# Expert stage of an attention and mixture-of-experts layer: the transposes of a tile's gated rows move behind the gate products of the next tile

## What is computed

```python
g = jnp.einsum('td,edf->etf', x, w_gate)
u = jnp.einsum('td,edf->etf', x, w_up)
h = jax.nn.silu(g) * u
down = jnp.einsum('etf,efd->etd', h, w_down)
routed = jnp.einsum('te,etd->td', gates, down)
shared = jax.nn.silu(x @ sw_gate) * (x @ sw_up) @ sw_down
out = routed + shared
```

## Time and profile before

| | us |
|---|---|
| median of 3 runs | 2293.08 |
| lowest, highest | 2290.29, 2299.49 |
| profiled execution | 2301.97 |
| its span, first to last instruction | 2300.3 |
| TensorE busy in the span | 2139.7 (93%) |
| VectorE busy | 1483.7 (64%) |
| ScalarE busy | 1034.7 (45%) |
| mean granted TensorE clock | 0.974 of full speed |

### The profile page before, as it was taken

One profiled execution on the slowest core, in us unless ns is written; L12 is line 12 of the kernel. 1 busy time (PEld: TensorE's weight loads), 2 busy tenths in 40 slices (PEclk: granted clock), 3 DMA queues, 4 the chain that ended last, 5 costly groups with the idle time before them and its releaser, 6 DMA issues. The chain is left out here.

```text
span 2300.3 us, 32737 instructions
## 1 busy us (share of the span) xinstructions
PE 2139.7 (93%) x11865; PEld 1389.3 (60%) x11865; DVE 1483.7 (64%) x3323; ACT 1034.7 (45%) x1924; POOL 1168.6 (51%) x717
## 2 busy tenths in 40 slices
PE   6999899999999999999999988699998899999997
PEld 5777544444444444444444432577776798999896
DVE  3665786767767677777777760765657556565654
ACT  3333255555555555555555555322222334443433
POOL 1010166557465674656746557455563345465554
PEclk9999799999999999999999999899999899999999
DMA  5678711412213122161231200344432676767673
GB/s 169 233 264 257 194 31 38 93 33 69 67 38 93 29 67 72 38 153 29 68 71 38 73 17 19 124 147 129 147 111 80 235 242 196 237 227 249 215 225 115
DMA packets 172913, 283.69 MB, mean 123 GB/s; under 512 B 28622, under 2 KB 75214, under 8 KB 172752
## 3 DMA queue, kind: packets, MB, share of 16 engines
q1 hardware_dynamic: 151488, 219.09, 32.5%
q0 software_dynamic: 21264, 62.51, 8.2%
HBM read 196.22 MB, written 86.90 MB: 123 GB/s over the span
## 5 line engine op out<-in xcount | busy, mean ns | idle before, releaser
L931 ACT ACTIVATE b_pt<-b_st 128x512 f32<-128x512 f32 (+3 forms) x1280 | 612.5, 535 | 472.7 <-DVE b_st L893 187.6
L752 POOL TENSOR_TENSOR b_acc<-b_acc,b_pt 128x1024 f32<-128x1024 f32 (+1 forms) x256 | 592.9, 2346 | 214.3 <-ACT b_pt L931 213.7
L871 DVE TENSOR_REDUCE b_mpart<-b_mx 128x1 f32<-128x512 f32 x768 | 512.1, 686 | 184.8 <-PE b_mx L988 182.1
L1011 PE MATMUL b_st<-b_q,b_k 97*128 97x512 f32 (+2 forms) x1280 | 497.4, 402 | 57.5 <-ACT b_pt L931 54.0
L988 PE MATMUL b_mx<-b_k,b_q 96*128 96x512 f32 (+2 forms) x1280 | 508.9, 412 | 6.9 <-DVE b_mpart L871 3.3
L988 PEld LDWEIGHTS b_mx<-b_k,b_q 96*128 96x128 f32 x1280 | 248.4, 195 | 262.0 <-DVE b_mpart L871 148.9
L1011 PEld LDWEIGHTS b_st<-b_q,b_k 97*128 97x128 f32 x1280 | 242.3, 191 | 262.7 <-ACT b_pt L931 237.4
L1024 PE MATMUL b_ob<-b_pt,b_v 128*32 128x512 f32 (+3 forms) x2560 | 303.6, 547 | 1.1 <-ACT b_pt L931 1.1
L868 DVE CUSTOM_DVE_ANT_0 b_unread<-b_mx,b_later 128x384 bf16<-128x384 f32 (+3 forms) x512 | 244.5, 484 | 87.0 <-PE b_mx L988 86.3
L752 POOL TENSOR_TENSOR b_acc<-b_pt 128x1024 f32<-128x1024 f32 x48 | 113.5, 2379 | 263.0 <-ACT b_pt L931 263.0
L80 PE MATMUL c_fb<-e_w_split,e_xh 128*128 128x352 f32 x408 | 142.3, 349 | 1.4 <-DVE e_xl L1727 1.4
(11 more groups left out here) (296 smaller groups left out, 3818.0 us busy)
## 6 DMA issues: line engine op xcount, KB each, us to landing
b_q<-scr_qh SPq DMA_DIRECT2D x64, 256.0 KB, 4.5
b_k<-scr_kh SPq DMA_DIRECT2D x64, 256.0 KB, 4.1
sw_raw<-in_L_ffn_w_gate_dram SPq DMA_DIRECT2D x14, 704.0 KB
sw_raw<-in_L_ffn_w_up_dram SPq DMA_DIRECT2D x14, 704.0 KB
c_x_rows<-in_L_ffn_w_gate_dram SPq DMA_DIRECT2D x13, 704.0 KB
c_x_rows<-in_L_ffn_w_up_dram SPq DMA_DIRECT2D x13, 704.0 KB
a_xin<-in_L_attn_x_dram POOLq DMA_DIRECT2D x8, 1024.0 KB, 5.8
scr_qh<-wo SPq DMA_DIRECT2D x8, 1024.0 KB, 5.0
```

The lines of the kernel that those rows point to most:

```text
L752: g.tensor_tensor(out[:, :, lo:], so_far[:, :, lo:], pt[n % NPB][:, :, lo:], ALU.add).then_inc(s_add, 1)
L871: v.tensor_reduce(part, mxb[i % NMX][:, 0:w], AX.X, ALU.max).then_inc(s_red, 1)
L931: act.activation(pt[n % NPB][:, j, lo:], stb[:, (2 * n + j) % NST, lo:], ACT.Exp, scale=SCALE).then_inc(s_exp, 1)
L1011: pe.matmul(stb[:, (2 * n + j) % NST, lo:], kb[:, h, at:at + P], qb[:, h, q * CH + lo:(q + 1) * CH], start=True, stop=True).then_inc(s_st, 1)
```

## The change

The transposes of the gated rows of tile i-1 are issued behind the gate product of tile i, ahead of the transposes of the input rows of tile i+1, and no longer ahead of that gate product. For the last tile they stand where they stood. ScalarE's silu of tile i waits in addition for c_hf of tile i-1, and the gate product of tile i waits in addition for silu of tile i-1. No instruction is added or removed. Line numbers behind the edits are up to 6 higher.

```diff
         for i in range(UNITS):
             act.wait_ge(s_g, i + 1)
+            if i:
+                act.wait_ge(s_h, i)
             act.activation(sg, gb[:, 0:F], ACT.Silu).then_inc(s_sg, 1)
...
         for i in range(UNITS):
             pe.wait_ge(s_xl, i + 1)
+            if i:
+                pe.wait_ge(s_sg, i)
             hidden(gb, i, 0).then_inc(s_g, 1)
+            if i:
+                turn_hidden(i - 1)
             if i + 1 < UNITS:
                 pe.wait_ge(s_x[(i + 1) % UNDER_WAY], turns(i + 1, UNDER_WAY))
                 turn_row(pe, begun, keep, i + 1).then_inc(s_t, 1)
             hidden(ub, i, 1).then_inc(s_u, 1)
             if i:
                 down_row(i - 1)
-            turn_hidden(i)
+        turn_hidden(UNITS - 1)
         down_row(UNITS - 1)
```

## The result

| | before | after |
|---|---|---|
| median of five runs, us | 2293.08 | 2315.51 |
| lowest, highest | 2290.29, 2299.49 | 2309.01, 2324.65 |
| profiled execution: time, span | 2301.97, 2300.3 | 2324.65, 2322.9 |
| expert stage in the profile (first gate product to last down product) | 498.4 | 521.9 |

The account below looks back on a forecast made before the run. TensorE was taken to bound the expert stage. New waits of 30.3 us, less 7.5 gone, plus 0.7 at tile 6, gave 23.5 us longer: 2316.6 us on the median, range 2301 to 2334.

Parts of the forecast that it names:

- both pieces: Tiles with both late weight pieces and one addition: slack 0.53 to 0.57, each 1.44 short, 7.2 us of new waits.
- three additions: Six tiles with three additions and an up piece: slack 0.3 to 1.0, together 7.6 us of new waits.
- two additions and a piece: Five tiles with two additions and a down piece: slack 1.45, short by 0.56 each, 2.8 us of new waits.
- five others: Tiles 27, 49, 66, 68 and 70: slack 1.2 to 1.8, together 3.0 us of new waits.
- seven with late output rows: Tiles 15, 19, 26, 37, 48, 52, 59, where an addition waits for output rows: 9.7 us of new waits.
- Tile 6: Tile behind the one wait for a weight transfer: e_xl ends at 1836.7, making it 0.7 us longer.
- The waits gone: TensorE's waits for c_hf at nine places besides tile 6 vanish, saving about 7.5 us.
- The waits only go: VectorE catches up between c_hl and e_xl; c_hf waits vanish, none come: near -6, 2287 us; chance 0.04.
- Under half of it: Output rows' arrivals don't move and each shift is 0.3 us smaller: about +9, 2302 us; chance 0.09.
- The clock falls at seven transposes in a row: TensorE product takes 3.56 us instead of 2.00 in up to 70 tiles: +109, 2402 us; chance 0.02.
- Weights come late as well: Weight fetches, issued about 2 us later, bring 12 more waits of 2: +24 more, 2341 us; chance 0.05.
- It does nothing: The change has no effect because e_xl is not on the chain; chance 0.02.

Follow-up runs that it names:

- e6: Changed kernel with the gated rows' transposes behind 3 of the gate product's 12 matmuls; ratio 1.0009 to the kernel before.
- e7: Kernel before with only the two added waits, transposes in their old place; ratio 0.9981 to the kernel before.
- e12: Kernel before with only the weight pieces of the block of index 3 split two tiles later; ratio 0.9965 to the kernel before.
- e5: Changed kernel with the gated rows' transposes behind 6 of the gate product's 12 matmuls; ratio 1.0007 to the kernel before.
- e8: Changed kernel with additions and late pieces behind e_xl, and block 3's pieces two tiles later; ratio 0.9981 to the kernel before.

## Why the prediction was right, point by point

**Right in its mechanism and its sum, partly by compensation.** The waits moved from c_hf to e_xl, and the undisturbed tile did not change. By the steps of the prediction, in us of waits for e_xl, start to start:

| kind of tile | forecast | measured |
|---|---|---|
| both pieces (five) | 7.2 | 7.0 |
| three additions (six) | 7.6 | 6.0 |
| two additions and a piece (five) | 2.8 | 2.6 |
| five others | 3.0 | 1.1 |
| seven with late output rows | 9.7 | 8.3 |
| together | 30.3 | 25.0 |

- *Five others* was mis-sized: tiles 27, 49 and 66 do not wait. In the trace of the kernel before, c_hh of the tile but one before had started 1.40, 1.61 and 0.90 us after its transposes, on an idle ScalarE, and not 0.53. So the slack was read too small by 0.87, 1.08 and 0.37. The line for tile 27, whose transposes start at 1977.88:

```profile
1979.28 0.49 ACT L2015 ACTIVATE c_hh<-e_tb 128x384 fp32r<-128x384 f32 x1 [3.35 <-PE e_tb L2065]
```

  In the changed kernel these three start at the usual distance, and e_xl is 0.25, 0.25 and 0.18 us early, as a slack of 2.2 less 2.00 says. There the semaphore of the transposes was raised late, 0.02 us ahead of c_hh; why, the trace does not show.
- *Three additions* was mis-sized in the same way at tiles 21 and 54, where c_hh had started 0.91 and 0.97 us after its transposes. Five of the six wait 0.97 or 0.98, as a slack of 1.0 says, and tile 65 waits 1.16.
- *Late rows.* Tile by tile: 15 forecast 1.85, measured 1.17; 19: 2.8 and 3.1; 37: 1.0 and 1.1; 48: 0.4 and 0.1; 52: 2.0 and 2.3; 59: 1.3 and 0.5; 26: 0.3 and 0. That an earlier wait lets the rows catch up is borne out, also at tile 32, put among those with three additions: forecast 1.7 from its own late row, measured 0.97 like its kind.
- *Tile 6.* Its e_xl ended at 1835.39, not at 1836.7, but this stage also began 1.08 us earlier. Counted from the first gate product, e_xl ended 1.3 us later than before, against 1.5 forecast, and the gate product started 0.3 later, against 0.5.
- *The waits gone.* Behind tile 6 the rows of the kernel before give 7.0 us at eight places, and tile 0 gives 0.84. The 7.5 for nine places therefore seem to hold tile 0, whose 0.8 is already in the delay of tile 6: some 0.5 to 0.8 us are counted twice.
- *The clock.* It was taken to cost nothing new, and cost about 2.5 us more (the products of tiles 6, 19 and 52 against those of 6 and 19). The product behind the wait of tile 52 ran at 0.56; before, after a wait of 1.9 there, at 1.00. The stretches are the down product with its wait, and the gate product behind it (columns as in the earlier trace rows):

```profile
2165.30:2169.67 4.37, 2.27 (x11) 1.51 (x10) 1.40 (x3) 0.00 (x0) 0.00 (x0) 1.00 0.96 315
2169.67:2173.03 3.36, 3.36 (x13) 3.29 (x13) 0.37 (x1) 0.00 (x0) 2.57 (x3) 0.56 0.29 73
```

- *The restart.* The sum counts a wait only with the time that TensorE stands idle. But a gate product behind a wait takes 2.02 us (1915.33 to 1917.35 above), and one right behind the down product 1.92 (1990.31 to 1992.23). That is 0.10 more at each of 27 waits, 2.7 in all, less 0.05 at each of nine waits before, where the transposes took 0.30 and not 0.25: 2.2 us.

So the waits were 5 us fewer than forecast, and the clock, the weights' wait (7.2 instead of 6.9) and the restart gave back 5. In the whole stage 29.1 us of waits for e_xl, tiles 4 to 6 included, less 10.6 for c_hf gone, and 2.5, 0.3 and 2.2 make 23.5 of the 23.6. That the errors cancel is luck.

**The rivals.** *The waits only go* fell: it needed a shift below the slack, and e6 shows what such a shift does: its time is not told from no change. *Under half of it* fell with 23.6. *The clock falls at seven transposes in a row* fell too, in this stretch of one tile, from gate product to gate product:

```profile
1983.49:1990.31 6.82, 6.82 (x42) 6.40 (x41) 5.58 (x7) 3.88 (x5) 5.18 (x4) 1.00 0.40 140
```

The clock is at 1.00 with the seven inside, and its mean over the span is 0.973, where it was 0.974. The Trainium skill's rule (TensorE: Matmul & The Clock Gate, Part 4: PE-mode transpose) costs nothing here, among products; what it does to transposes alone, no run here shows. *Weights come late as well* did not happen beyond the first wait, but for 0.6 us once on ScalarE. *It does nothing* is out.

**The costs put at nothing.** The added waits: shown by e7. The cover of c_hl, 1.0 us: no wait for c_hl is new in the changed kernel.

## What to carry to other kernels

Moving work later on the busiest engine moves everything that hangs on it, on every list behind it; read for each consumer how much slack it has, and compare it with the shift tile by tile, since the mean tells nothing (most tiles here had room, 26 had not). Read the slack in more than one tile of a kind: some single tiles here were late in one execution and not in the next. A list on another engine is right only for one order of the busiest: putting additions and pieces behind e_xl takes half a per cent off the changed kernel and costs 2% in the old one. And work for which nothing in the chain waits belongs into the engine's idle time and not between two links.

## What the runs showed of the hardware

A wait of TensorE can be followed by products near half clock, and its length alone does not decide it. In the changed kernel the gate product behind a wait of 2.3 us had 0.56 and the one behind 3.1 us 0.50; before, one of 2.7 us was followed by 0.52 and one of 1.9 us by 1.00. But in e6, 0.84 us behind a wait of 1.9 the clock stood at 0.51, and in e12 it stayed at 1.00 behind one of 2.7:

```profile
2154.86:2157.59 2.73, 2.73 (x12) 2.67 (x10) 1.88 (x3) 1.95 (x3) 1.66 (x2) 0.51 0.53 195
```

```profile
1917.18:1919.70 2.52, 2.52 (x18) 2.50 (x19) 0.56 (x1) 0.52 (x2) 1.80 (x3) 1.00 0.15 42
```

Transposes next to products of another kind cost no time for the change of kind: three and four apart take 0.25 and 0.36 us of TensorE's starts and the gate product 2.00; seven together take 0.33 and 0.36, and the gate product ahead of them is 0.08 shorter, 1.92. The sum is 2.61 both times. A gate product behind a wait takes 2.02 again.

The high part c_hh starts 0.53 us after its transposes in most tiles, but in single tiles of five kernels (the one before, e5, e6, e7 and e8) 0.9 to 3.0 us after them. ScalarE is idle then, and the semaphore of the transposes is raised just ahead of c_hh; why so late is open.
